# Layer 1 of a two-layer transformer kernel: three side jobs of the tensor engine moved to other eighths of a slot

## What is computed

```
x1 = layer0(x);  xn = layernorm(x1)
# attention of layer 1: 16 heads of 16 channels, 2 batches, 1024 positions
Xn = LN(xn) * ln_w + ln_b;  q, k, v = split(Xn @ W_in);  q, k = rope(q), rope(k)
probs = softmax(q @ k.T / 4)
att = (probs @ v) @ W_out + xn
# a feed-forward that works on the 64 tokens of each batch that the router ranks highest
out = x1 + att + routed_ffn(xn)
```

## Time and profile before

| | us |
|---|---|
| median of 3 runs | 1046.46 (1044.51 to 1050.87) |
| the profiled execution, its time | 1043.54 |
| its span in the trace | 1041.7 |
| slots 5 to 40 of layer 1 (from the first maximum reduction) | from 679.3 on |
| a slot without Y and Z | 9.53 |
| a slot with Y or Z | 10.63 |

### The profile page before, as it was taken

One profiled execution on the slowest core, in us unless ns is written; L12 is line 12 of the kernel. 1 busy time (PEld: TensorE's weight loads), 2 busy tenths in 40 slices (PEclk: granted clock), 3 DMA queues, 4 the chain that ended last, 5 costly groups with the idle time before them and its releaser, 6 DMA issues.

```text
span 1041.7 us, 26416 instructions
## 1 busy us (share of the span) xinstructions
PE 917.6 (88%) x8703; PEld 509.5 (49%) x8703; DVE 855.8 (82%) x1760; ACT 684.2 (66%) x1779; POOL 704.2 (68%) x1034
## 2 busy tenths in 40 slices
PE   3588898998998998998998997689999999999998
PEld 2355666665665765666665665342222222323223
DVE  6798778888888888788788786578999999899871
ACT  2555656655565665665565555127999999888885
POOL 3668878887888888888888878432766765444221
PEclk9799999999999999999999999879999999999999
DMA  5556644454444444444544444243221132222101
GB/s 195 128 115 131 106 96 78 96 99 82 90 98 82 90 99 81 92 98 83 96 97 82 86 90 91 44 134 65 60 43 23 23 41 42 52 43 46 28 1 42
DMA packets 247995, 82.57 MB, mean 79 GB/s; under 512 B 222196, under 2 KB 246452, under 8 KB 247604
## 3 DMA queue, kind: packets, MB, share of 16 engines
q1 hardware_dynamic: 247428, 78.53, 37.7%
q10 hardware_dynamic: 432, 2.36, 0.7%
HBM read 18.49 MB, written 4.19 MB: 22 GB/s over the span
## 4 chain that ended last, share of the span: by engine, by line
POOL 41%; issue 19%; DVE 18%; PE 17%; DMA 2%; SPq 1%; ACT 1%; POOLq 0%; DVEq 0%; ACTq 0%
DVE l_mxv L1333 17%; POOL rm L743 15%; POOL t L752 10%; POOL t L769 9%; PE l_mx L1535 6%; PE l_acc L1506 5%; POOL rs L743 2%; POOL tcw L788 1%; PE l_sc L1566 1%; POOL r L832 1%; PE l_sc L1543 1%; POOL r L830 1%; POOL xl L808 1%; DMA qkv_all<-w_qkv 1%; DMA ats<-an 1%
## 5 line engine op out<-in xcount | busy, mean ns | idle before, releaser
L1333 DVE TENSOR_REDUCE l_mxv<-l_mx 128x1 f32<-128x1024 f32 x256 | 295.1, 1215 | 26.9 <-PE l_mx L1535 26.2
L1246 ACT ACTIVATE l_prob<-l_sc 128x512 f32<-128x512 f32 x512 | 273.2, 604 | 18.0 <-PE l_sc L1543 16.7
L427 ACT ACTIVATE an<-an 128x256 f16<-128x256 f32 x128 | 53.3, 416 | 203.9 <-DVE an L601 203.8
L752 POOL TENSOR_TENSOR t<-t 128x320 f32<-128x320 f32 x128 | 110.5, 863 | 109.7 <-DVE t L648 109.6
L1535 PE MATMUL l_mx<-early 48*128 48x512 f16 x512 | 156.3, 387 | 20.3 <-DVE l_mxv L1333 14.3
L1543 PE MATMUL l_sc<-early 50*128 50x512 f16 x512 | 156.3, 383 | 0.3 <-ACT l_prob L1246 0.3
L743 POOL TENSOR_TENSOR rm<-ss,half_neg 128x5 f32<-128x5 f32 x128 | 156.5, 1223 | 0.0
L1506 PE MATMUL l_acc<-l_prob,qkv_all 128*17 128x256 f32 x2048 | 155.0, 387 | 0.0
L922 PE MATMUL ob<-wo_hi,ats 128*128 128x256 f16 x512 | 106.0, 275 | 33.6 <-DMA ats<-an 29.1
L880 PE MATMUL qk<-early,xh 128*128 128x384 f16 x512 | 130.2, 337 | 3.8 <-issue 3.4
L867 PE MATMUL pv<-v,probs 128*64 128x65 f32 x2048 | 89.0, 230 | 29.2 <-ACT probs L476 22.3
(11 more groups left out here) (187 smaller groups left out, 2058.7 us busy)
## 6 DMA issues: line engine op xcount, KB each, us to landing
qkv_all<-w_qkv SPq DMA_DIRECT2D x3, 768.0 KB, 9.1
v<-v SPq DMA_DIRECT2D x64, 32.5 KB, 2.0
xn_all<-xs SPq DMA_DIRECT2D x16, 128.5 KB, 2.1
xa<-x SPq DMA_DIRECT2D x16, 128.0 KB, 2.4
tk<-nat SPq DMA_TRANSPOSE x128, 2.8
qkv_all<-w_o SPq DMA_DIRECT2D x8, 256.0 KB, 3.7
ats<-an SPq DMA_TRANSPOSE x128, 2.5
xc<-x SPq DMA_DIRECT2D x16, 128.0 KB, 2.4
```

The lines of the kernel that those rows point to most:

```text
L427: return act.activation(dst, src, ACT.Copy, scale=scale)
L752: pool.tensor_tensor(t1[:, b, :, :], t1[:, b, :, :], t2[:, :, :], ALU.add).then_inc(s_["pool_u"], 1)
L1246: act.activation(prob[:, (y * NI + u) % NPR, h * 512:(h + 1) * 512], sc[:, k % NSC, :], ACT.Exp, scale=D1 ** -0.5).then_inc(s_["act_sc"], 1)
L1333: dve.tensor_reduce(mxv[:, x % 2, u:u + 1], mx[:, MX[k] % 2, :], AX.X, ALU.max).then_inc(s_["dve_mx"], 1)
```

## The change

Three numbers move. Y and Z go from u = 3 to u = 2 (`OUT_U` and `AHEAD_AT`; two more of Z's places in slot 38 go from 1 and 4 to 2 and 5). M goes from u = 4 to u = 3 (`ROW_U`). F goes from u = 4 to u = 6 (`FOLD_U`). ScalarE's and VectorE's parts of these jobs move with them. The first M waits for `hid0s` and no longer for `hid1s`, as one half less of the hidden layer stands ahead of it.

```diff
-AHEAD_AT = ((33, 3), (34, 3), (35, 3), (36, 3), (37, 2), (37, 5), (38, 1), (38, 4))
+AHEAD_AT = ((33, 2), (34, 2), (35, 2), (36, 2), (37, 2), (37, 5), (38, 2), (38, 5))
...
-COPY_U, FOLD_U = 1, 4
+COPY_U, ROW_U, FOLD_U, OUT_U = 1, 3, 6, 2
...
-            if u == 4 and 0 <= c - LAG_M < ITEMS:
+            if u == ROW_U and 0 <= c - LAG_M < ITEMS:
                 order.append(("M", c - LAG_M))
...
-            if u == 3 and 0 <= c - SLOT_Y < NI:
+            if u == OUT_U and 0 <= c - SLOT_Y < NI:
                 order.append(("Y", c - SLOT_Y))
...
                         if t == 0:
-                            pe.wait_ge(s_["mod_act"], MOD["hid1s"])
+                            pe.wait_ge(s_["mod_act"], MOD["hid0s"])
```

More of the change, by code:

```diff
@@ L1248, in _ @@
                     t = c - LAG_M
-                    if u == 4 and item(t):
+                    if u == ROW_U and item(t):
                         k = SC["M", t]
@@ L1335, in _ @@
                     i = c - SLOT_Y
-                    if u == 3 and 0 <= i < NI:
+                    if u == OUT_U and 0 <= i < NI:
                         k = ("Y", i)
```

## The result

| | before | changed |
|---|---|---|
| median of the comparison's runs (4 each) | 1046.56 us (1044.51 to 1050.87) | 1065.75 us (1053.86 to 1068.28) |
| span of the profiled execution | 1041.7 | 1065.3 |
| its mean granted clock on PE | 0.975 | 0.963 |

The ratio is 1.015 (1.0105 to 1.0194): slower by over 1%, where 1051 us (1042 to 1057) was forecast. One of the four changed runs, 1053.86 us, lies inside the range, and three lie at 1064 to 1068. Ratios here leave out executions that took over 1.5% more than the fastest of their kernel; medians are over all of them.

A forecast was written before the change was run, and what follows sets the result against it. Handovers among PE, VectorE and ScalarE, all nearly full, were taken to bound each slot. Plain slots +5.6, slots with Y or Z +1.2 and a vanished DMA -0.5 gave +6.3 us on 1045: 1051 us, range 1042 to 1057.

The forecast's parts named there:

- The ring at E(4,1): Eighth 4's second score matmul waits one exponential later, for E(3,1); taking M and F out of eighth 4 gains only 0.04 us.
- F at 0.37 in eighth 6: F, moved between a piece and a maximum matmul, adds 0.37 us of pure PE work to eighth 6, all counting.
- The lower price: F adds only 0.25 us in eighth 6, if it follows the piece as smoothly as M does; sum +2.9 us.
- A plain slot of 9.86 us: Slots without Y and Z go from 9.53 to 9.86 us, +0.33 each, +5.6 us over 17 slots.
- With Y: In 12 slots of 10.63 us, Y's move gains 0.27 and F takes 0.37: +0.10 a slot, +1.2 us in all.
- The late DMA before slot 21: M's one late DMA, before eighth 0 of slot 21, disappears as its rows come earlier: -0.5 us.
- (a): Even spread works: slots fall to VectorE's pace, 9.05 us, total 1024; chance 0.06 for over 1%, 0.04 for less.
- (b): The ring doesn't bite at E(4,1), as ScalarE's exponentials come earlier: -1.5 us, 1043.5; chance 0.13.
- (c): F's copy on ScalarE makes E(7,1) wait for E(6,1) in 29 slots: +10.7 us in all, 1056 and up; chance 0.12.
- I start from 1045: Base time for the sum, as the profiled 1043.54 us lay at the lower end of runs with median 1046.46.
- 1 us or so for the spread of the runs: Margin added at each end of the range, beyond rival totals of 1043.5 and 1056 us.
- Slots 5 to 7 move M only ... 0 give or take 0.3: Slots 5 to 7, where M moves beside waits for VectorE, were put at no change, within 0.3 us.

## Why the prediction was wrong

- **The ring at E(4,1)** (forecast: eighth 4 gains 0.04 us and no more): right. T5 is T1 + 5.12 against 5.10, the matmul of line 1543 is 0.34 behind its twin, and M alone costs the whole 0.33 us a slot. With eighth 3 longer by a piece the wait is gone, and a slot is 9.52 us again.
- **F at 0.37 in eighth 6**: right, the upper of the two prices. F starts 0.56 behind its piece, where M, behind its own, starts 0.45 after it. The maximum matmul, with 128 columns as F and float16 as M, takes the longer step too, so the width fits as the reason for the 0.11 us; no run varies the width alone. The rule of the Trainium skill that changing the tiling mode drains the engine (TensorEngine Tiling (Array Packing), Key Properties) agrees with this trace. The lower price did not occur: F costs 0.37 here and not 0.25.
- **A plain slot of 9.86 us**: measured 9.86. **With Y**: 10.78 for 10.73. T3 comes 0.05 us later than reckoned, and the end of eighth 4 with it. Alone, Y's move gains 0.03 where 0.11 was expected; with M's new number it meets the wait of 0.22 at E(4,1).
- **The late DMA before slot 21**: gone from the chain, as said, and from every profile with M in eighth 3. But its 0.5 us belongs to the one profile that I read: with M and the pieces in their old places that slot was longer by 0.5, 0.1, 0.5, 0.1 and 0 us in five profiles (a sixth, with the tripled matmuls, has another slot 1.4 us long). Slots 8 to 35 together are +6.6 us, where the terms of the forecast give +6.2.
- **Rivals.** (a) is refuted by the holes at 772.63 and 775.19, (b) by the 0.34 us at E(4,1); eighth 4 lasts 1.87 us and not 1.53. (c) does not occur: no wait at E(7,1) makes slots longer than 9.86. The price of over 1% that (c) carried came by another way, which I had not listed.
- **The step that failed** is the start of the sum and the width of the range: "I start from 1045", and "1 us or so for the spread of the runs", with "Slots 5 to 7 move M only ... 0 give or take 0.3". Three runs from 1044.51 to 1050.87 looked like a kernel with a spread of a few microseconds. Over 107 runs it spans 22 us, and the middle one is at 1051.4. In place of 0, slots 5 to 7 measured +12.6 us in the profiled pair, and the code ahead of them, which is identical and had no term in the sum, +4.1; in a second execution of the changed kernel they measured +1.5 and +0.7. The largest part that the profiles show is made in slots 5 and 6: the page of before had the dip in its clock line, 13.7 us at half clock, and I read it as a fact of the kernel and not as one throw of a die. In the comparison, three of four changed runs were long (79 to 98 us at half clock by their mean clocks, one of them seen in a profile) and no run of before was; that gave +19 us for a change that is worth +6.4. Against 35 runs of before the change measures 1.0018 (0.9983 to 1.0054), which, on the other side, is less than its slots say, and for the same reason.

Open: why the clock takes 13.7 us in one execution and 41.0 in another of the same program, and whether three long runs among the first four were chance. Only the tripled matmuls moved it dependably, by the mean clocks of their six runs, and they made it longer.

## What to carry to other kernels

A side job that takes a number in a ring of buffers shifts every later wait in that ring: here it cost 0.33 us a slot, by a wait that stands nowhere in the diff. A second move can turn a harmless new number into a wait, as Y's did with M's, so single moves don't price a pair. Where an engine's eighths are uneven, even out the work that holds no buffer of the ring (the value pieces: 9.53 to 9.45 us) and leave the side jobs.

Before forecasting a run's time, look for stretches at half clock in the one profile; each can be a part of the spread between runs, at about 0.4 us for each us of it here. Judge a change of half a per cent by the length of its slots in two profiles, or by many runs set against their clock, not by the medians of four.

## What the runs showed of the hardware

- PE busy for 20.00 of 20 us, three windows in a row, did not bring the full clock: with maximum matmuls of 48 rows, three times as many, the granted clock stayed at 0.50 for 61 us. With one matmul over 128 rows added ahead of each, in place of the tripling, it was back at 1.00 within 20.5 and 13.7 us in the two profiles. That the rows are the reason is not shown: the same kernel without them has 13.7 us too.
- The same program had 13.7 us at half clock in one execution and 41.0 in another, and two executions of 12.9 us difference had the same slots from 8 on.
